# A graph kernel: the last column group of the pair sort shared between scatter and products, and an output stage with one vector product per tile

## The reference, cut to what matters

```python
x = layernorm(x + L0(x, src, dst))              # agg = segment_sum(x[src], dst); two dense layers
x = layernorm(x + L1(x, src, dst))              # two SAGE layers
x = layernorm(x + L2(x, edge_weight, src, dst)) # weighted sums
x = layernorm(x + L3(...))                      # messages with filters, summed by node into agg
...
# the end of L3: agg is nodes x 8*128
S = agg[:, :2 * F] @ (W1_s / sqrt(2 * F))
V = einsum('nmi,mc->nci', agg[:, 2 * F:8 * F].reshape(n, 2 * F, 3), W1_v) / sqrt(2 * F)
S = shifted_softplus(S) @ (W2_s / sqrt(C))
V = einsum('nci,cd->ndi', V, W2_v) / sqrt(C)
out = concatenate([S, V.reshape(n, 3 * C)], axis=1)
# layernorm: (x - mean) / sqrt(var + 1e-5)
```

## Time and profile before

| | |
|---|---|
| Median of 3 runs | 2298.2 us (2297.6 to 2298.75) |
| The profiled execution's own time | 2299.14 us |
| Its span, first to last instruction | 2297.3 us |
| Mean granted TensorE clock | 0.914 of full speed |
| PE busy | 2055.8 us, 89% of the span |
| DVE busy | 1574.3 us, 69% |
| POOL busy | 1251.2 us, 54% |
| ACT busy | 1132.1 us, 49% |

### The profile page before, as it was taken

The page is one execution under the profiler, slowest core; times in us unless marked ns, Lnnn a source line. Parts: engine busy times, 40 slices in busy tenths (PEclk is TensorE's granted clock), DMA queues, the critical chain, the costliest instruction groups (busy, mean ns, idle before and its releaser), DMA issues.

```text
span 2297.3 us, 37124 instructions
## 1 busy us (share of the span) xinstructions
PE 2055.8 (89%) x7761; PEld 1167.5 (51%) x7761; DVE 1574.3 (69%) x4534; ACT 1132.1 (49%) x3234; POOL 1251.2 (54%) x1510
## 2 busy tenths in 40 slices
PE   4798961887888999999999799999999999999986
PEld 3454531665564555455444455555555555555545
DVE  8998752888886160110403488888888888888885
ACT  0396642777772010000010366666666666666654
POOL 1478874000004888888885356666666666666530
PEclk9598985667768999999999899999999999999998
DMA  5413020000002111121120133333333333333321
GB/s 195 155 14 88 3 69 16 0 0 0 0 0 62 39 43 21 21 62 20 20 62 14 67 98 98 100 99 101 97 97 97 99 100 101 97 97 98 98 66 45
DMA packets 75077, 146.99 MB, mean 64 GB/s; under 512 B 26829, under 2 KB 37570, under 8 KB 74631
## 3 DMA queue, kind: packets, MB, share of 16 engines
q0 software_dynamic: 44704, 95.66, 16.8%
q1 hardware_dynamic: 27356, 45.20, 5.9%
q10 hardware_dynamic: 2946, 5.28, 0.6%
HBM read 123.11 MB, written 22.40 MB: 63 GB/s over the span
## 4 chain that ended last, share of the span: by engine, by line
PE 70%; POOL 10%; DVE 10%; issue 6%; DMA 2%; DVEq 1%; ACT 1%; ACTq 0%; SPq 0%; POOLq 0%
PE ps L898 24%; PE ps L641 11%; POOL pair_table L526 10%; PE ps L660 8%; PE ps L789 5%; PE ps L836 4%; PE ps L881 3%; PE ps L883 3%; PE ps L882 3%; PE ps L884 3%; DVE adj_t L1217 1%; PE ps L788 1%; DVE dense L1406 1%; DVE dense L1405 1%; DMA pair_table<-dense 1%
## 5 line engine op out<-in xcount | busy, mean ns | idle before, releaser
L898 PE MATMUL ps<-adj_t 128*128 128x512 f32 x1288 | 615.3, 600 | 14.0 <-DVE adj_t L1643 14.0
L1109 ACT ACTIVATE adj_t<-adj_t 128x128 f32<-128x128 f32 x966 | 315.4, 389 | 211.0 <-DVE adj_t L1622 209.9
L582 POOL DMA_INDIRECT adj_t<-z_table,adj_t x322 | 309.6, 962 | 154.0 <-DVE adj_t L1632 68.4
L898 PEld LDWEIGHTS ps<-adj_t 128*128 128x128 f32 x1288 | 231.3, 189 | 249.6 <-issue 215.0
L526 POOL DMA_INDIRECT pair_table<-dense x192 | 236.6, 1232 | 130.5 <-issue 119.8
L540 POOL DMA_INDIRECT src_table<-st_two,src_rows x216 | 261.1, 1209 | 70.4 <-issue 65.2
L789 PE MATMUL ps<-dense 128*128 128x128 f32 x832 | 246.4, 416 | 0.0
L660 PE MATMUL ps<-wring,dense 128*128 128x512 f32 (+1 forms) x480 | 210.0, 600 | 4.6 <-issue 3.2
L533 POOL DMA_DIRECT2D st_two<-records x54 | 31.9, 591 | 329.1 <-DVE adj_t L1430 328.9
L788 PE MATMUL ps<-dense 128*128 128x128 bf16 x416 | 111.8, 269 | 110.7 <-ACT dense L1044 70.6
L881 PE MATMUL ps<-dense_r 128*128 128x512 f32 x322 | 200.3, 622 | 2.3 <-POOL dense_r L590 2.3
(11 more groups left out here) (274 smaller groups left out, 3786.3 us busy)
## 6 DMA issues: line engine op xcount, KB each, us to landing
src_table<-dense SPq DMA_DIRECT2D x8, 656.0 KB, 6.6
adj_t<-z_table,adj_t POOLq DMA_INDIRECT x322, 3.4
records<-dense SPq DMA_DIRECT2D x1, 5000.0 KB
adj_t<-src_table SPq DMA_DIRECT2D x73, 64.0 KB, 1.8
adj_t<-zeros SPq DMA_DIRECT2D x1, 4576.0 KB
src_table<-st_two,src_rows POOLq DMA_INDIRECT x216, 2.6
st_two<-records POOLq DMA_DIRECT2D x54, 62.5 KB, 2.1
adj_t<-zeros SPq DMA_DIRECT2D x1, 3328.0 KB, 12.1
```

The costliest lines, as they stand in the source:

```text
L582: g.indirect_dma_start(out=zg[:, s, c, :], out_offset=None, in_=z_table, in_offset=bass.IndirectOffsetOnAxis(ap=dsti[:, s, c:c + 1].bitcas ...
L898: last = mm(bank[6 + h], oh[:, c, :], msg[:, c, h * D:(h + 1) * D], start=c == c0, stop=c == c0 + count - 1)
L1109: last = A(msg[:, c, (2 + k) * P:(3 + k) * P], msg[:, c, MSG:MSG + P], ACT.Copy, scale=side[:, s, c, C_Y - ATT + k:C_Y - ATT + k + 1])
```

## The change

Three things are changed.

1. The last column group (number 9) is shared: its first 16 columns stay with the scatters (176 columns in all), its last 16 join the products (144). `split_places` makes both forms of the places for this group, with a wait between them.
2. The output stage forms W12 = W1_v W2_v once at the start of L3 (two transposes and two products on PE, two copies on ACT, the second written over `w1v`). A tile's vector output is then one product of the sums with W12: six 128-column products with the sums as the stationary operand, written where the outputs are read; `outputs` keeps its scalar product only. ACT no longer copies the vector part.
3. Tiles are normalised one by one. DVE adds epsilon per tile. For tiles 0 to 7 ACT makes a first value of the inverse root by Ln and Exp (`root`) and POOL refines it by a Newton step of four small operations; for tiles 8 and 9 ACT uses Sqrt and DVE a reciprocal. DVE normalises tile t-1 behind `finish(t)`. SP, no longer ACT, issues the ten stores.

```diff
-DMA_COLS = [t * LJ + c for t in DMA_BLOCKS for c in range(LJ)]
-PERM_COLS = [j for j in range(EJ) if j // LJ not in DMA_BLOCKS]
+SHARED = BLOCKS_J - 1
+DMA_COLS = [t * LJ + c for t in DMA_BLOCKS for c in range(LJ // 2 if t == SHARED else LJ)]
+PERM_COLS = [j for j in range(EJ) if j not in DMA_COLS]
...
+        w1vT = aT[:, 0, 0:2, :]
...
+            for t in range(NT):
+                sp_eng.wait_ge(y_ready, t + 1)
+                sp_eng.dma_start(out[t * P:t * P + rows_of(t), :], xa[0:rows_of(t), t, :]).then_inc(out_done, 16)
+            sp_eng.wait_ge(out_done, 16 * NT)
...
+            for t in range(NT - 2):
+                pool.wait_ge(guessed, t + 1)
+                r, w = rstd[:, t:t + 1], rtmp[:, t:t + 1]
+                link(g.tensor_tensor(w, r, r, ALU.mult))
+                link(g.tensor_tensor(w, w, stat[:, 1, t:t + 1], ALU.mult))
+                link(g.tensor_scalar(w, w, -0.5, 1.5, ALU.mult, ALU.add))
+                g.tensor_tensor(r, r, w, ALU.mult).then_inc(refined, 1)
...
             pe.wait_ge(l3w_ready, 2)
+            for k in range(2):
+                last = nc.tensor.transpose(bank[6][:, k * P:(k + 1) * P], w1v[:, k, :], ident[:, :])
+            last.then_inc(wT_done, 1)
             for s in range(2):
                 attrs_T(0, s)
                 filter_in(0, s)
+            pe.wait_ge(wT_copied, 1)
+            for k in range(2):
+                last = mm(bank[7][:, k * P:(k + 1) * P], w1vT[:, k, :], w2sv[:, 1, :], start=True, stop=True)
+            last.then_inc(w12_done, 1)
+            pe.wait_ge(w12_ready, 1)
             filter_out(0, 0, 0)
...
-                for k in range(2):
-                    last = mm(svbank[s][:, P:D], w1v[:, k, :], aT[:, s, 2 + 3 * k:5 + 3 * k, :].rearrange("p m n -> p (m n)"),
-                              start=k == 0, stop=k == 1)
                 last.then_inc(sv_done, 1)
+                if t >= 2:
+                    pe.wait_ge(o_read, t - 1)
+                for m in range(3):
+                    for k in range(2):
+                        last = mm(obank[s][:, (1 + m) * P:(2 + m) * P], aT[:, s, 2 + 3 * k + m, :], w1v[:, k, :], start=k == 0, stop=k == 1)
+                last.then_inc(v_done, 1)
...
-                for m in range(KT):
-                    last = mm(obank[s][:, m * P:(m + 1) * P], svT[:, s, m * P:(m + 1) * P], w2sv[:, 0 if m == 0 else 1, :], start=True, stop=True)
-                last.then_inc(o_done, 1)
+                mm(obank[s][:, 0:P], svT[:, s, :], w2sv[:, 0, :], start=True, stop=True).then_inc(o_done, 1)
...
             nc.scalar.preload_act_table_set("natural_log_exp_and_others")
+            act.wait_ge(wT_done, 1)
+            A(w1vT, bank[6][:, 0:2 * P].rearrange("p (k n) -> p k n", k=2), ACT.Copy).then_inc(wT_copied, 1)
             attrs(0, 0)
             softplus_exp(0, 0)
             softplus_log(0, 0)
             attrs(0, 1)
+            act.wait_ge(w12_done, 1)
+            A(w1v, bank[7][:, 0:2 * P].rearrange("p (k n) -> p k n", k=2), ACT.Copy).then_inc(w12_ready, 1)
             hidden_hi(0, 0)
...
+            def root(t):
+                r = rows_of(t)
+                act.wait_ge(var_ready, 3 * NT + t + 1)
+                if t < NT - 2:
+                    link(A(rstd[0:r, t:t + 1], stat[0:r, 1, t:t + 1], ACT.Ln))
+                    A(rstd[0:r, t:t + 1], rstd[0:r, t:t + 1], ACT.Exp, scale=-0.5).then_inc(guessed, 1)
+                else:
+                    A(rstd[0:r, t:t + 1], stat[0:r, 1, t:t + 1], ACT.Sqrt).then_inc(std_ready, 1)
...
-                A(svT[:, s, P:D], sv[:, P:D], ACT.Copy).then_inc(act_sv, 1)
...
-            act.wait_ge(var_ready, 3 * NT + 1)
-            A(stat[:, 1, :], stat[:, 1, :], ACT.Sqrt).then_inc(std_ready, 1)
-            for t in range(NT):
-                act.wait_ge(y_ready, t + 1)
-                act.dma_start(out[t * P:t * P + rows_of(t), :], xa[0:rows_of(t), t, :]).then_inc(out_done, 16)
-            act.wait_ge(out_done, 16 * NT)
+                if t >= 2:
+                    root(t - 2)
+            root(NT - 2)
+            root(NT - 1)
...
-                else:
+                if by_products:
+                    if by_dma:
+                        dve.wait_ge(rows_ready[s], DMA_BLOCKS.index(t) + 1)
...
             activated(0)
             for t in range(NT):
                 if t + 1 < NT:
                     activated(t + 1)
                 finish(t)
-            v.tensor_scalar(stat[:, 1, :], stat[:, 1, :], EPS, None, ALU.add).then_inc(var_ready, 1)
-            dve.wait_ge(std_ready, 3 * NT + 1)
-            link(v.reciprocal(stat[:, 1, :], stat[:, 1, :]))
-            for t in range(NT):
-                y = xa[0:rows_of(t), t, :]
-                r = rows_of(t)
-                v.tensor_scalar(y, y, stat[0:r, 0, t:t + 1], stat[0:r, 1, t:t + 1], ALU.subtract, ALU.mult).then_inc(y_ready, 1)
+                if t:
+                    normalised(t - 1)
+            normalised(NT - 1)
```

More of the change, by code:

```diff
@@ L248, in build @@
         bf2_r = dense_r[:, NT * D + 3 * N + P:NT * D + 3 * N + P + D]
-        svT = T1[:, 1, 0:2 * D].rearrange("p (s n) -> p s n", s=2)
+        svT = T1[:, 1, 0:2 * P].rearrange("p (s n) -> p s n", s=2)
+        w1vT = aT[:, 0, 0:2, :]
+        rstd, rtmp = [T1[:, 1, 2 * P + 16 * k:2 * P + 16 * k + NT] for k in range(2)]
         assert at[0] <= 2 * AW_COLS
@@ L346, in build @@
         t_done, aT_ready, sv_done, svT_ready, o_done, o_read = sem("t_done"), sem("aT_ready"), sem("sv_done"), sem("svT_ready"), sem("o_done"), sem("o_read")
-        act_sv = sem("act_sv")
+        act_sv, v_done, guessed, refined = sem("act_sv"), sem("v_done"), sem("guessed"), sem("refined")
+        wT_done, wT_copied, w12_done, w12_ready = sem("wT_done"), sem("wT_copied"), sem("w12_done"), sem("w12_ready")
         y_ready, out_done = sem("y_ready"), sem("out_done")
@@ L957, in mixed @@
                 for k in range(2):
-                    mm(svbank[s][:, 0:P], w1s[:, k, :], aT[:, s, k, :], start=k == 0, stop=k == 1)
-                for k in range(2):
-                    last = mm(svbank[s][:, P:D], w1v[:, k, :], aT[:, s, 2 + 3 * k:5 + 3 * k, :].rearrange("p m n -> p (m n)"),
-                              start=k == 0, stop=k == 1)
+                    last = mm(svbank[s][:, 0:P], w1s[:, k, :], aT[:, s, k, :], start=k == 0, stop=k == 1)
                 last.then_inc(sv_done, 1)
+                if t >= 2:
[4 more added lines that the diff above has]
+                last.then_inc(v_done, 1)
             def outputs(t):
@@ L966, in outputs @@
                 pe.wait_ge(svT_ready, t + 1)
-                if t >= 2:
-                    pe.wait_ge(o_read, t - 1)
-                for m in range(KT):
-                    last = mm(obank[s][:, m * P:(m + 1) * P], svT[:, s, m * P:(m + 1) * P], w2sv[:, 0 if m == 0 else 1, :], start=True, stop=True)
-                last.then_inc(o_done, 1)
+                mm(obank[s][:, 0:P], svT[:, s, :], w2sv[:, 0, :], start=True, stop=True).then_inc(o_done, 1)
             sums_T(0)
@@ L1175, in sums @@
                 if t >= 2:
-                    act.wait_ge(sv_done, t - 1)
+                    act.wait_ge(v_done, t - 1)
                 for h in range(2):
                     A(aT[:, s, 4 * h:4 * h + 4, :].rearrange("p m n -> p (m n)"), bank[4 * s + h], ACT.Copy).then_inc(aT_ready, 1)
+            def root(t):
[6 more added lines that the diff above has]
+                    A(rstd[0:r, t:t + 1], stat[0:r, 1, t:t + 1], ACT.Sqrt).then_inc(std_ready, 1)
             sums(0)
@@ L1186, in _ @@
                 if t >= 2:
-                    act.wait_ge(o_done, t - 1)
                     act.wait_ge(svT_ready, t - 1)
                 sv = bank[2 + 4 * s]
-                A(svT[:, s, P:D], sv[:, P:D], ACT.Copy).then_inc(act_sv, 1)
                 spt = sp[:, s * P:(s + 1) * P]
@@ L1266, in places, with split_places @@
                 v.tensor_reduce(pos_f[:, n * L:(n + 1) * L], pv.rearrange("p (a b) -> p a b", b=B), AX.X, ALU.add).then_inc(pos_step[s], 1)
-            def split_places(s, t, by_dma):
+            def split_places(s, t, by_dma, by_products):
                 j = slice(t * LJ, (t + 1) * LJ)
@@ L1355, in _ @@
                 if (n + 1) * STEP % LJ == 0:
-                    split_places(PAIR, n * STEP // LJ, n * STEP // LJ in DMA_BLOCKS)
+                    split_places(PAIR, n * STEP // LJ, n * STEP // LJ in DMA_BLOCKS, n * STEP // LJ in PERM_BLOCKS + [SHARED])
                 if n * STEP // LJ == 1 and (n + 1) * STEP % LJ == 0:
@@ L1380, in _ @@
                 places(SRC, t, LJ)
-                split_places(SRC, t, True)
+                split_places(SRC, t, True, False)
                 one_hots(4)
@@ L1667, in activated @@
                 s = t % 2
-                dve.wait_ge(act_sv, 2 * t + 2)
+                dve.wait_ge(act_sv, t + 1)
+                if t >= 2:
+                    dve.wait_ge(o_done, t - 1)
```

(10 more changed lines are left out.)

## The result

The changed kernel took 2284.64 us (median of 5; 2275.41 to 2290.75), the kernel before 2297.6 (2296.66 to 2298.75): ratio 0.9943, 95% interval 0.9925 to 0.9961. That is 13 us faster where 31.8 were forecast, and outside the range of 2262 to 2273. The spread tells as much as the median: 2 us before, 15 after.

What follows compares the result with a forecast made beforehand. Bounds: POOL's scatters end the pair sort, PE the L3 loop and output stage. Terms -23.9 + 0.5 + 1.3 - 7.6 - 2.1 = -31.8 us, from 2298.2 to 2266.4; forecast 2263.5 to 2269 (0.64), wider range 2262 to 2273 (0.91).

Steps and rivals of the forecast that it cites:

- So the columns cost nothing while 11 us of cover remain: Pair sort: sixteen added product columns fit into DVE's 49.8 us wait for the table, costing 0 us.
- Rival one: Pair sort: products become the bound, from 1.6 us per added column, at half clock; 2.1 to 5 us more; chance 0.09.
- Scatters: Pair sort: sixteen scatters less at 1.491 us save 23.9 us; slower POOL beside busy DVE costs 0.5.
- W12 at the start of L3: Start of L3: forming W12 delays POOL's L590 and PE's next work, +1.3 us, bounds 0 and 2.0.
- The L3 loop: L3 loop: PE has no idle time, so it moves whole, its own time unchanged and the delay not given back.
- Output loop: Output stage: 3.0 us per tile for 3.50, bounds 2.88 and 3.50; seven steps give 3.5 us.
- the last finish: End of the output stage: DVE's finish of the last tile starts 3.8 us earlier.
- one normalisation for ten: Behind the last finish: one normalisation of 0.54 us replaces ten in 4.65, gain 3.8 us.
- rival two: Output loop keeps 3.5 us per tile because root and refinement hold up DVE and PE; 2270 to 2271 us; chance 0.13.
- Stores: End of the span: only the last store follows the end, 2.6 us for 4.7, -2.1; bounds 0 and -2.4.

Runs made afterwards that it cites:

- a1: The kernel before, run again unchanged in the first follow-up set: 2295.73 us.
- a2: The changed kernel, run again unchanged in the first follow-up set: 2263.49 us.
- c1: The kernel before, unchanged, profiled beside the changed one in a set with the short place phase: 2296.99 us.
- c2: The changed kernel, unchanged, in a set with the short place phase: 2258.05 us.
- d1: The kernel before, unchanged, in a set with the long place phase: 2297.51 us.
- d2: The changed kernel, unchanged, in a set with the long place phase: 2274.14 us.
- f1: The changed kernel with the column sharing undone and 67 memsets on DVE ahead of the merge: 2285.20 us, ratio 0.9945.
- e2: The kernel before with 67 one-column memsets on DVE ahead of the merge, inside its wait: 2291.04 us.
- set A: Runs made together on one chip: both kernels again (2295.73 and 2263.49 us), and each half of the change alone (2289.15 and 2270.36).
- sets A and C: Two groups of runs made together, both with the short place phase; the changed kernel took 2263.49 and 2258.05 us.
- set D: Both kernels unchanged, run together some minutes after the preceding set on the same chip, long place phase: 2297.51 and 2274.14 us.
- f3: The changed kernel, unchanged, in the last set, long place phase: 2278.41 us, ratio 0.9913.
- b1: The changed kernel, unchanged, timed in five rounds beside the kernel before: 2279.42 us, ratio 0.9919.

## Why the prediction was wrong, point by point

The change of the profiled spans, us, each pair from one set (the first pair from two profiles not taken together). The marks are the first L1431, the last addition of the block loop, the first and last hidden_hi (L1141), the last L1711 and the last start of L1727, and their like before:

```
                              forecast  first pair     a1,a2     c1,c2     d1,d2
start of the merge               -23.4        +4.4     -21.2     -22.9      -7.4
block loop behind it               0          -5.5      -5.3      -5.4      -5.4
from there to the start of L3    +1.3        +2.4      +3.5      -1.2      -1.3
L3 loop                            0          -1.6      -1.1      -1.3      -1.2
to the last finish               -3.8        -3.7      -3.8      -3.7      -3.7
to the last normalisation        -3.8        -3.9      -3.9      -3.9      -3.9
to the end of the span           -2.1        -0.6      -0.6      -0.6      -0.6
sum                             -31.8        -8.5     -32.4     -39.0     -23.5
```

- **The step that failed:** "So the columns cost nothing while 11 us of cover remain". The 49.8 us under it were read from one execution and taken as a property of the kernel. In d1 they are 17.0, in f1 17.5, in e2 12.7 (in the last two 67 memsets take 1.5 of them). With d1's 17.0 the forecast's own terms (23.9 for the scatters, 15.1 for the columns) make the products 22 us late; d2's merge is 16.6 us behind the 361.3 at which its table would have allowed it (385.3 - 24.0), the columns being cheaper (11.8) and its cast 2.1 earlier. What makes a set's place phase long, and so the cover small, stays open. The working was right, its input not. Nor is -32.4 in set A a hit: the merge gained 2.2 less there, the way to L3 2.2 and the stores 1.5 less than forecast, and shorter loops that nobody forecast (5.3 and 1.1) paid for it.
- **Rival one** named the event, products as the bound of the sort, at 0.09, but by another mechanism (half clock for the added columns) and at 2.1 to 5 us. From the cast to the point where DVE is free, the columns cost 10.8 to 14.2 for sixteen in sets A and C and 11.8 in set D, below the forecast's 15.1, but 15.7 in the first pair and some 18 between f1 and f3. Half clock is not the cause there: in the first profile of after, ten columns from 338.09 on take 8.79 us, with a granted clock of 1.00 from 338 to 347. With the late phase ahead of them, the products cost 17 us of the gain in set D and 30 in the first profile (390.5 against 386.2 - 25.4).
- **Scatters:** the last one starts 21.0, 23.2 and 24.0 us earlier in sets A, C and D, for 23.4. The Trainium skill ("SBUF — State Buffer", Who interferes with whom) has DVE's two-port forms lock GpSimd out for the whole instruction. By that rule the forecast estimated a loss of up to 14 us. No pair shows more than 2.8 (set A, 21.0 for 16 x 1.491 = 23.9).
- **W12 at the start of L3:** +1.3 was forecast, and that is what it cost. POOL's first gather out of `z_table` and its `hidden_lo`, in the kernel before and then in the changed one:

```profile
1311.03 1.02 POOL L582 DMA_INDIRECT adj_t<-z_table,adj_t  x1 [13.49 <-DMA z_table<-dense]
...
1315.85 1.27 POOL L590 TENSOR_TENSOR dense_r<-adj_t,dense_r 128x512 fp32r<-128x512 f32 x1
```

```profile
1310.15 1.03 POOL L590 DMA_INDIRECT adj_t<-z_table,adj_t  x1 [13.18 <-DMA z_table<-dense]
...
1316.37 1.26 POOL L598 TENSOR_TENSOR dense_r<-adj_t,dense_r 128x512 fp32r<-128x512 f32 x1 [1.42 <-ACT dense_r L1141]
```

From the one to the other pass 4.8 us in each of the four profiles of before, 6.2 in the first of after and in a2, 6.0 in c2 and d2; POOL now waits for ACT. So +1.2 to +1.4. In the table it is drowned, because the same changed kernel takes 604.4 us from block loop to L3 in c2 and 608.9 in a2. Most of these 4.5 us lie where PE runs at a lower granted clock. In the ten us from 125 us behind the loop's last addition it is 0.78 and then 0.88 in a2 and 1.00 in both halves in c2, and two groups of the chain take 1.7 us more. They are, in a2 and then in c2:

```profile
806.81 2.25 PE ps L667 x12
809.06 2.98 PE ps L824 x6
```

```profile
805.30 1.43 PE ps L667 x12
806.74 2.12 PE ps L824 x6
```

Two more such places, at the start (0.68 for 0.94 from 3 to 6 us behind the loop) and at 455 to 460 us (0.61 for 1.00), bring another 0.8 and 1.3. Why the clock was granted later in a2 is open.
- **The L3 loop** gives back little: its row counts from ACT's first `hidden_hi`, and PE's first product behind it starts 2.2 us later where it was 3.0. Counted from that product (L881, L897) the loop is 0.4 to 0.8 us shorter.
- **Output loop:** 3.0 forecast, 3.04 measured; the last finish 3.7 earlier for 3.8, one normalisation for ten 3.9 for 3.8. PE does not wait for ACT's root or POOL's refinement anywhere in it, so rival two did not happen.
- **Stores:** -2.1 forecast, -0.6 measured. I priced the last store by the one of z_table, 2.27 us; from the end of the last L1727 (2284.64) to the end of the span pass 4.2 us, not 2.6. The last traffic lies between 2286.3 and 2286.6; the last 2.2 us of the span show none. In the kernel before it goes on to between 2296.3 and 2296.6, and only the last 0.7 us show none. So the transfer was not longer than told, and a longer tail came behind it, which the trace does not explain.
- **Missing:** the block loop's -5.3 to -5.5. It was in no term and no rival, and is why sets A and C came out at 2263.5 and 2258.1, near the low end of the range and below it, while those with the long phase came out above its range (d2 at 2274.1, b1, f3 and the first result at medians of 2278 to 2285).

## What to carry to other kernels

A wait that hides work is only as large as the smallest one over several executions: when a change spends 39 of 50 us of cover, profile the kernel before more than once first, at different times, and look at marks well ahead of the wait, since equal times say nothing of a phase that is hidden. Where indirect DMAs run beside a stretch of many small instructions, take that stretch's length as uncertain: here its end moved from 204.8 to 241.3 us. And when a loop changes its time with the same data and the same body, count the instructions ahead of it before looking for a cause in the change.

## What the runs showed of the hardware

- The same program, beside indirect scatters from POOL at one per 1.49 us, had one of two kinds of place phase, with the same 65 small matmuls and 400 place products: cast at 202 to 207 us or at 233 to 247. All profiles of a set agreed; the same chip had both. With the scatters moved away it was at 202.6 in a set with the long kind and at 199.8 in one with the short.
- In the long kind PE, ACT and DVE show waits for "issue" and "remote" that no semaphore in the trace explains: in d1 from 90 to 240 us 13.1, 13.7 and 9.5 us, in c1 none. PE's come at half the pitch of the scatters.
- 67 one-column memsets on DVE took 1.5 us in all, and 5.4 us off a loop of 416 blocks behind them (316.2 in d1, 310.8 in e2).
- The same changed kernel took 604.4 and 608.9 us for its middle; of the 4.5 us, 3.8 lie in three places where the granted clock was 1.00 or 0.94 in one and 0.61 to 0.88 in the other.
